# The end of the attention cores and the start of the projection, in a fused eight-stage transformer kernel

## The reference, cut to what matters

```python
for n in 0..3:
    x = x + tanh(g_xattn[n]) * xattn_n(layernorm(x), ctx, ...)
    x = x + tanh(g_ffn[n])   * ffn_n(layernorm(x), ...)
```

```python
scores = einsum('bhsr,bhlr->bhsl', q_r, k_r)        # l: 1500 keys
attn   = softmax(scores, axis=-1)                   # a sum over the keys divides
ctx_c  = einsum('bhsl,bld->bhsd', attn, kv_rope)
out    = einsum('bhsd,hkd->bshk', ctx_c, w_kc_kv).reshape(b, s, H * K) @ Wo.T
```

## Time and profile before

| | |
|---|---|
| median of the runs | 2488.33 us |
| profiled execution | 2486.28 us |
| its span (first to last instruction) | 2484.5 us |
| PE busy | 2277.2 us, 92% |
| DVE busy | 1557.1 us, 63% |
| POOL busy | 1431.8 us, 58% |
| ACT busy | 1043.9 us, 42% |
| mean granted TensorE clock | 0.935 |

### The profile page before, as it was taken

One profiled execution on the slowest core, in us unless ns is written; L12 is line 12 of the kernel. 1 busy time (PEld: TensorE's weight loads), 2 busy tenths in 40 slices (PEclk: granted clock), 3 DMA queues, 4 the chain that ended last, 5 costly groups with the idle time before them and its releaser, 6 DMA issues. The chain is left out here.

```text
span 2484.5 us, 31100 instructions
## 1 busy us (share of the span) xinstructions
PE 2277.2 (92%) x11508; PEld 1580.0 (64%) x11508; DVE 1557.1 (63%) x2538; ACT 1043.9 (42%) x1522; POOL 1431.8 (58%) x870
## 2 busy tenths in 40 slices
PE   6889999899999976698999999879997999999878
PEld 5677887766666652565566666467886566666567
DVE  4566653377878757765787887442224787878432
ACT  3434443355555524211455555323332555554332
POOL 0442200188888872266688888734442788888733
PEclk9889998799999986698899999879998999999879
DMA  1025563111111013001111111022211111110010
GB/s 34 20 76 157 180 193 98 50 38 57 38 56 38 26 51 112 29 1 38 38 38 52 43 38 44 1 73 83 83 33 51 38 38 56 38 56 26 1 54 22
DMA packets 49842, 136.48 MB, mean 55 GB/s; under 512 B 7469, under 2 KB 13437, under 8 KB 49244
## 3 DMA queue, kind: packets, MB, share of 16 engines
q1 hardware_dynamic: 49308, 134.16, 17.6%
q10 hardware_dynamic: 384, 0.33, 0.1%
HBM read 121.26 MB, written 13.21 MB: 54 GB/s over the span
## 5 line engine op out<-in xcount | busy, mean ns | idle before, releaser
L2139 DVE TENSOR_REDUCE mx<-psum 128x1 f32<-128x500 f32 x1008 | 652.4, 675 | 231.9 <-PE psum L1232 219.6
L1662 ACT ACTIVATE E<-psum 125x896 f32<-125x896 f32 x576 | 528.2, 920 | 586.7 <-PE psum L1253 559.3
L1906 POOL TENSOR_TENSOR SA<-SA,E 125x896 f32<-125x896 f32 x288 | 609.7, 2117 | 22.6
L1261 PE MATMUL psum<-E,V 125*64 125x448 f32 x2304 | 471.7, 545 | 0.0
L1232 PE MATMUL psum<-K,Q 128*128 128x500 f32 x1008 | 358.9, 411 | 20.8 <-ACT Q L1649 11.2
L1251 PE MATMUL psum<-Q,K 128*125 128x448 f32 x1152 | 331.7, 369 | 2.3 <-ACT E L1662 2.3
L1253 PE MATMUL psum<-Q,K 128*125 128x448 f32 x1152 | 329.8, 367 | 0.0
L1261 PEld LDWEIGHTS psum<-E,V 125*64 125x64 f32 x2304 | 152.9, 136 | 231.0 <-issue 223.4
L1232 PEld LDWEIGHTS psum<-K,Q 128*128 128x128 f32 x1008 | 189.0, 191 | 166.0 <-issue 45.4
L1906 POOL TENSOR_TENSOR SA<-SA,SB 125x896 f32<-125x896 f32 x96 | 200.3, 2086 | 157.8 <-DVE SB L2160 157.8
L1251 PEld LDWEIGHTS psum<-Q,K 128*125 128x125 f32 x1152 | 213.0, 187 | 36.7 <-ACT E L1662 6.9
(11 more groups left out here) (294 smaller groups left out, 3731.9 us busy)
## 6 DMA issues: line engine op xcount, KB each, us to landing
K<-kt_scratch SPq DMA_DIRECT2D x48, 750.0 KB, 4.9
K<-kt_scratch SPq DMA_DIRECT2D x48, 375.0 KB, 6.0
EW<-in_f_w SPq DMA_DIRECT2D x64, 256.0 KB, 6.6
kt_scratch<-kt SPq DMA_DIRECT2D x16, 750.0 KB, 4.3
WS<-in_f_w SPq DMA_DIRECT2D x31, 384.0 KB, 4.7
WoT<-in_a_WoT SPq DMA_DIRECT2D x24, 256.0 KB, 2.6
V<-in_ctx SPq DMA_DIRECT2D x16, 375.0 KB
Wq<-in_a_Wq SPq DMA_DIRECT2D x16, 256.0 KB, 3.1
```

Source lines behind the costliest of these rows:

```text
L1261: i = e.matmul(psum[c * DC:(c + 1) * DC, 4 + b % 2, 0:HT], V[0:LP, b, k * DC:(k + 1) * DC], E[g[n, b, k] % NE][0:LP, half[c]], start=k == ...
L1662: e.activation(E[m % NE][0:LP, :].rearrange("p (c q) -> p c q", c=2), psum[0:LP, pair:pair + 2, 0:HT], ACT.Exp).then_inc(exp_set.sem, 1)
L1906: e.tensor_tensor(SA[b % 2][0:LP, :], a[0:LP, :], x[0:LP, :], ALU.add).then_inc(sum_set.sem, 1)
L2139: e.tensor_reduce(mx[:, b % 2, j * 3 + c:j * 3 + c + 1], psum[:, bank, 0:CW], AX.X, ALU.max).then_inc(small_free.sem, 1)
```

## The change

1. **The last batch's sum.** For the last batch POOL adds only up to block 7 (`LAST_ADDED`). The task `total` of this batch is moved from the end of the list to behind `add` 9, which on PE's queue is behind the `values` of block 7 and ahead of those of 8 to 11. There PE multiplies four tiles with ones in place of one, adding up in PSUM: SA, SB (blocks 8+9), and the E of blocks 10 and 11. It waits for the sum up to 7, for the pair and for the last exponential.
2. **The first tile's parts.** In layers 1 to 3, ACT makes the high part and POOL the low part of tile 0 at the end of the core, ahead of the barrier. ACT waits for the scores of batch 14 and the division of batch 2, as CH 0 and CL 0 now lie where the key tiles of batches 13 and 14 were, and tile 0 holds the tokens of batches 0, 1 and part of 2.
3. **The low parts shared.** In layers 0, 2 and 3 the low parts of the odd tiles (1, 3, 5) are done by DVE. In layer 1 POOL does all.

```diff
+LAST_ADDED = 7
@@ core_order
                 if (phase, n) == (1, 2):
                     order += [("div", b - 1)] if b > 0 else []
                     order.append(("add", b, 9))
+                    order += [("total", b)] if b == B - 1 else []
-    order += [("values", B - 1, NL - 1)]
-    return order + [("total", B - 1), ("div", B - 1)]
+    return order + [("values", B - 1, NL - 1), ("div", B - 1)]
@@ build
-    CH = [mem.take("CH", [P, H // 2, P], F32R) for _ in range(3)]
-    CL = [mem.take("CL", [P, H // 2, P], F32R) for _ in range(3)]
+    CH = [mem.take("CH", [P, H // 2, P], F32R)]
+    at(top + (4 * L + 31) // 32 * 32)
+    CH.insert(0, mem.take("CH", [P, H // 2, P], F32R))
+    CL = [mem.take("CL", [P, H // 2, P], F32R)]
+    assert mem.at <= after_k1
+    CH.append(mem.take("CH", [P, H // 2, P], F32R))
+    CL += [mem.take("CL", [P, H // 2, P], F32R) for _ in range(2)]
+    def by_pool(b, k):
+        return k in ADDED and (b < B - 1 or k <= LAST_ADDED)
+    def low_by_pool(n, i):
+        return n == 1 or i % 2 == 0
@@ pe_core, total
-                e.wait_ge(*sum_set.at(n, b, NL - 1))
-                for c in range(2):
-                    i = e.matmul(psum[c * DC:(c + 1) * DC, bank, 0:HT], ones[0:LP, 0:DC], SA[b % 2][0:LP, half[c]], start=True, stop=True)
+                terms = [SA[b % 2]]
+                if b < B - 1:
+                    e.wait_ge(*sum_set.at(n, b, NL - 1))
+                else:
+                    e.wait_ge(*sum_set.at(n, b, LAST_ADDED))
+                    e.wait_ge(*pair_set.at(n, b, 9))
+                    e.wait_ge(*exp_set.at(n, b, NL - 1))
+                    terms += [SB[1], E[g[n, b, 10] % NE], E[g[n, b, 11] % NE]]
+                for x in terms:
+                    for c in range(2):
+                        i = e.matmul(psum[c * DC:(c + 1) * DC, bank, 0:HT], ones[0:LP, 0:DC], x[0:LP, half[c]],
+                                     start=x is terms[0], stop=x is terms[-1])
@@ pe_project
-            e.wait_ge(*cl_set.at(n, i))
+            e.wait_ge(*low_flag(n, i).at(n, i))
+    def act_part(e, n, i):
+        if i == 0 and n > 0:
+            e.wait_ge(*scored.at(n, B - 2, NL - 1))
+            e.wait_ge(*o_divided.at(n, 2))
+        if i >= 3:
+            e.wait_ge(*projected.at(n, i - 3))
+        e.activation(CH[i % 3][:, :, :], QR[:, :, tok(i)], ACT.Copy).then_inc(ch_set.sem, 1)
+    def low_part(e, n, i):
+        e.wait_ge(*ch_set.at(n, i))
+        e.tensor_tensor(CL[i % 3][:, :, :], QR[:, :, tok(i)], CH[i % 3][:, :, :].bitcast(F32),
+                        ALU.subtract).then_inc(low_flag(n, i).sem, 1)
@@ scalar_program / gpsimd_program
                 act_core(e, n)
+                act_part(e, n, 0)
                 pool_core(e, n)
+                low_part(e, n, 0)
@@ pool_project
+        if n == 0:
+            low_part(e, n, 0)
+        if low_by_pool(n, 1):
+            low_part(e, n, 1)
         for i in tiles:
+            if i + 2 < NT and low_by_pool(n, i + 2):
+                low_part(e, n, i + 2)
             pool_rstd(e, 1 + 2 * n, i)
@@ dve_project
+        if not low_by_pool(n, 1):
+            low_part(e, n, 1)
         for i in tiles:
+            if i + 2 < NT and not low_by_pool(n, i + 2):
+                low_part(e, n, i + 2)
             if turning and i >= 2:
                 dve_turn(e, r, i - 2, 4 + (i - 2) % 4)
```

More of the change, by code:

```diff
@@ L710, in build @@
     pair_set = flag("pair_set", per_core("add"))
-    sum_set = flag("sum_set", [e for e in per_core("scores") if e[2] in ADDED])
+    sum_set = flag("sum_set", [e for e in per_core("scores") if by_pool(*e[1:])])
     valued = flag("", per_core("values"), valued0)
@@ L716, in build, with low_flag @@
     out_tiles = [(n, i) for n in range(4) for i in tiles]
-    ch_set, cl_set, projected, x_out = (flag(n, out_tiles) for n in ("ch_set", "cl_set", "projected", "x_out"))
+    ch_set, projected, x_out = (flag(n, out_tiles) for n in ("ch_set", "projected", "x_out"))
+    def low_by_pool(n, i):
+        return n == 1 or i % 2 == 0
+    cl_pool = flag("cl_by_pool", [t for t in out_tiles if low_by_pool(*t)])
+    cl_dve = flag("", [t for t in out_tiles if not low_by_pool(*t)], out0_low)
+    def low_flag(n, i):
+        return cl_pool if low_by_pool(n, i) else cl_dve
     gate_w_set, logits_made = (flag(n, [(f,) for f in experts]) for n in ("gate_w_set", "logits_made"))
@@ L1670, in added @@
         return sum_set.at(n, b, max(k, 1))
-    def act_project(e, n):
[L1673 to L1679, removed]
+    def act_part(e, n, i):
[9 more added lines that the diff above has]
+                        ALU.subtract).then_inc(low_flag(n, i).sem, 1)
+    def act_project(e, n):
+        if n == 0:
+            act_part(e, n, 0)
+        act_part(e, n, 1)
         for i in tiles:
             if i + 2 < NT:
-                parts(i + 2)
+                act_part(e, n, i + 2)
             if n == 0 and i in (4, 5):
@@ L1888, in pool_core @@
                 lows = (n, b, 5)
-            elif kind == "scores" and t[0] in ADDED:
+            elif kind == "scores" and by_pool(b, t[0]):
                 k = t[0]
@@ L1917, in pool_project @@
     def pool_project(e, n):
[L1918 to L1923, removed]
+        if n == 0:
+            low_part(e, n, 0)
+        if low_by_pool(n, 1):
+            low_part(e, n, 1)
         for i in tiles:
-            if i + 2 < NT:
-                parts(i + 2)
+            if i + 2 < NT and low_by_pool(n, i + 2):
+                low_part(e, n, i + 2)
             pool_rstd(e, 1 + 2 * n, i)
```

## The result

The changed kernel took 2457.33 us in the median of four runs (2456.17 to 2462.62), the kernel before 2488.31 us (2487.76 to 2488.78) beside it: a ratio of 0.988, 95% interval 0.9863 to 0.9897, so 31 us less; the forecast was 28.3 us less, 2460.0, with a range of 2456 to 2468. The profiled execution took 2456.94 us (span 2455.2), 29.3 us less than that of before. The same changed kernel, run on two more chips, had medians of 2460.29 and 2460.04 us beside 2487.34 and 2486.92, so 27.05 and 26.88 us less. Its single runs lie up to 7 us apart, and such differences lie in stretches that the change doesn't touch. Of the kernel before there is one profile.

The account below looks back on a forecast made before the run. TensorE was busy 92% of the span, so only stretches where it waits could give much. Layer 0 +0.3, layer 1 -8.4, layer 2 -10.3 + 0.3, layer 3 -10.2: -28.3 us, so median 2460.0, range 2456 to 2468.

Parts of the forecast that it names:

- The sum by TensorE: End of layers 1 to 3's last core: four-term product replaces GpSimd's last adds; division 3.90 us earlier in layer 1, 4.69 in layer 3.
- Tile 0's parts: Layers 1 to 3: parts made before the barrier; TensorE starts 0.13 us after the division, X 3.03 us after its first product.
- The clock: Projection's tile 0: TensorE idles only about 0.8 us, keeping full clock; a fall would lose 1.8 us in layers 2 and 3.
- Rival (a): TensorE falls to the lower clock at the barrier: 2463.6 us, or 2473 with the sum's 16 records slow too; chance 0.09.
- Layer 1: VectorE waits for the first weight, landing 5.0 us after issue; its first reduction starts at 901.4, a gain of 8.4 us.
- VectorE's low parts: Odd tiles, layers 0, 2, 3: 1.27 us each, 3.6 if waiting for GpSimd; 0.3 us loss charged in layers 0 and 2.
- rival (b): VectorE's low parts are held behind GpSimd's, and TensorE waits for late Y in layers 0 and 2: 2468.5 us; chance 0.08.
- Rival (c): Slower than before: TensorE waits for all nine low parts that VectorE gets, 33 us, so 2493 us; chance 0.02.
- (d): The new wait on TensorE's queue is fulfilled late, values 8 to 11 move back, half of 13.3 us goes: 2466.7; chance 0.06.
- The sum: All layers together: +0.3 in layer 0, -8.4 in layer 1, -10.3 + 0.3 in layer 2, -10.2 in layer 3: -28.3 us.

Follow-up runs that it names:

- buffers aligned: Changed kernel with the moved CH and CL buffers 128 bytes further on, at multiples of 2048 bytes from buffer 1's place: 2455.0 us in a single run.
- part 1 undone: Changed kernel with GpSimd again adding all blocks of the last batch and a one-term product with ones at the end: 2474.84 us, ratio 0.9952.
- part 2 undone: Changed kernel with tile 0's high and low part back behind the barrier in layers 1 to 3: 2475.85 us, ratio 0.9957.
- the last division late: Changed kernel with VectorE making the last batch's reciprocal three times over, so the last division of layers 1 to 3 comes later: 2483.13 us, ratio 0.9983.
- the first weight's early load: Changed kernel with layer 1's first raw weight loaded before the barrier and reduced before tile 0's X, other ternary steps one tile sooner: 2459.99 us, ratio 0.9884.
- two tiles' more: Changed kernel with layer 1's first weight loaded and reduced early, and the three quantisations behind tiles 4, 5 and 6: 2457.71 us, ratio 0.9883.

## Why the prediction was right, step by step

- **The sum by TensorE.** Forecast 3.90, 4.68 and 4.69 us in layers 1 to 3; the reciprocal of the last batch follows that of batch 14 after 14.43, 14.43 and 14.42 us in place of 18.26, 19.03 and 19.04: 3.83, 4.60 and 4.62. Of the last two, 0.8 us each is the old product's lower clock (1.76 in place of 0.97 us). The 16 records start as reckoned, 2.31 us after the first values step (reckoned 2.25), and nothing is waited for; the margin of the pair was 0.63 us (2308.52 against 2309.15). Values 11 and the reciprocal end together, as reckoned (2315.34 and 2315.33); by these rows, a shorter reciprocal alone would bring nothing, which no run tried.
- **Tile 0's parts.** The distance from the division to X of tile 0 fell from 8.81 and 8.63 to 3.28 and 3.29 us (forecast 3.16). TensorE starts after 0.11 us (0.13), at the higher clock; mis-sized by 0.15 us is the way from the first product to X (3.18 in place of 3.03). The moved buffer has 0.03 of it (3.15 with the buffers aligned), and about 0.10 is the step from the first product to the second, which start 0.22 us apart (2316.16 and 2316.38) and not 0.118; why, no run shows.
- **The clock.** Right, and the experiments price it. Tile 0 took 1.3 to 2.3 us longer in each layer behind 3.83 us of idling (part 1 undone, one term's product and another 2.9 us of idling ahead of it), 4.50 us (part 2 undone) and 6.82 us (the last division late). Behind 0.83 us the granted clock is 1.00 and the products are 0.12 us apart. Rival (a) is out. The forecast had priced the clock at 1.8 us in layers 2 and 3 alone; layer 1 pays it as well, where X of tile 0 comes later than the first weight.
- **Layer 1.** Forecast that the landing would become the wait, with the first reduction 5.12 us after the division: 5.13. Gain to there 3.83 + 4.51 = 8.34, forecast 8.4.
- **VectorE's low parts.** 1.21 to 1.27 us, forecast 1.27, and 2.5 once beside GpSimd's (forecast 3.6 at worst). Charged with 0.3 us of loss in layers 0 and 2, they lost none: layer 0's seven X take 19.05 us as before. The 0.3 us were the push that low part 5 gives to what follows it. In layer 0 that part runs from 121.38 to 122.60, takes 1.22 us although GpSimd's exponent instruction is under way until 121.87, and the next instruction comes 3.10 us after the one of the tile before, where it was 3.06. The wait for the exponent, which the forecast put on VectorE, is seen on GpSimd: 1.51 in place of 0.65 us, with VectorE's part at 1.26 (layer 3, VectorE, then GpSimd):

```profile
2320.61 1.26 DVE L1713 TENSOR_TENSOR CL<-QR,CH 128x1024 fp32r<-128x1024 f32 x1
...
2320.77 1.51 POOL L1903 TENSOR_TENSOR rstd<-rstd,exponent 128x1 f32<-128x1 f32 x1
2323.61 0.65 POOL L1903 TENSOR_TENSOR rstd<-rstd,exponent 128x1 f32<-128x1 f32 x1 [1.33 <-DVE rstd L2059]
```

The prediction says of a gain from freeing GpSimd that no one waits for it, and that sharing gives nothing; part 3 gains 0.7 us in each of layers 2 and 3, since without it tile 1 is late behind GpSimd. Its own numbers held this (low part 1 on GpSimd ready at 3.6 us, wanted at 3.0), and its sum stays right, as it never charged that wait. The Trainium skill ("Perfetto Trace Analysis", section Optimizing Scalar/DVE Operations) warns that GpSimd and VectorE share a read port of SBUF, so that moving work between them may not help. The runs agree that the two hold each other up (2.52 against 1.23 us; 3.28 against 1.23 us), but it decided only where VectorE itself was the bound: rival (b) is out for this change, and the same meeting took the gain of the first weight's early load. Rival (c) has no row that speaks for it, and (d) is out by the 0.63 us of margin.
- **The sum.** 8.30 + 9.98 + 9.74 = 28.02 us in the stretches, forecast 8.4 + 10.0 + 10.2 less 0.3 in layer 0 = 28.3. Layer 3 is 0.4 short of the 10.16: 0.16 for the slower products of tiles 2, 3, 5 and 6 (the moved buffers), 0.12 for X of tile 0 behind the division (3.28 in place of 3.16), 0.07 for part 1, and 0.07 the distance of X of tiles 0 and 1, 2.77 us in the trace before and 2.84 now. Layer 2 agrees to 0.02 us by luck: it has the same shortfalls, and the 0.3 us charged to VectorE's parts didn't come. The 31 us between the medians on the first chip are luck too, as far as they go beyond the stretches' 28.0; the other two chips have 27.05 and 26.88.

## What to carry to other kernels

Where a chain goes through all engines one after another, look for work on it whose inputs are older than the chain's last step: three of GpSimd's adds and the first tile's split had been ready to be done elsewhere or earlier, and the gain was the links plus the clock that TensorE lost while it waited. Undo each part by itself before pricing it: here parts 1 and 2 shared the clock's term, 32.4 us when undone one at a time, while all three parts together bring 28.0. When VectorE's work is moved in time, look at what GpSimd does beside it at the new place.

## What the runs showed of the hardware that was not expected

- VectorE's scalar operation on 128x2048 takes 1.23 us, and 3.24 to 3.31 us if a GpSimd two-input operation is under way, ending 1.1 us after it. One tile's shift made one such meeting two; two tiles' more made it none. It goes the other way as well: GpSimd's low part takes 2.4 us, and up to 3.5 us when it meets a VectorE operation, and its 128x1 exponent 0.65 us, and 1.5 beside VectorE's low part.
- TensorE's products of 256 columns are 0.120 us apart in place of 0.118 in the tiles whose high part begins 6016 or 14208 bytes from the first buffer; at 6144 and 14336 bytes they are back. Tiles 1 and 4, whose low part alone had moved (by 1920 bytes), kept 0.118, so the low part's place by itself doesn't slow them. Which distance matters was not tried, and the aligned placing has a single run.
- How many of tile 0's products run at the lower clock differs between layers and runs with the same idling: after 6.8 us of it X of tile 0 came 2.03, 1.35 and 1.87 us later in the three layers. Likewise the four records of the old product with ones took 1.76, 1.62 or 0.97 us after the same 2.9 us of idling.
